# Local attention on one core: the projection moved behind a transpose and issued in two halves, the maxima one step earlier

## What is computed

```python
blk = mean of each 8 x 8 block                                   # 49 tokens
y_cmp = _mha(Q, blk, blk, ...); y_sel = _mha(Q, K_sel, K_sel, ...)   # K_sel: the 4 best blocks
# local attention: each pixel attends to its 7 x 7 neighbourhood
q = _lin(Q, wq_w[2], wq_b[2]);  k = _lin(patches, wk_w[2], wk_b[2]);  v = _lin(patches, wv_w[2], wv_b[2])
attn = softmax(einsum('bnhd,bnwhd->bnhw', q, k) * scale)
y_win = _lin(einsum('bnhw,bnwhd->bnhd', attn, v), pj_w[2], pj_b[2])
y = g[..., 0:1] * y_cmp + g[..., 1:2] * y_sel + g[..., 2:3] * y_win + Q
t = depthwise 3x3(_lin(y, pin_w));  x1, x2 = split(t)
out = _ln(y + _lin(gelu(x1) * x2, pout_w))
```

## Time and profile before

| | us |
|---|---|
| median of 3 runs | 847.04 (840.56 to 847.26) |
| the profiled execution | 846.81 |
| its span | 845.0 |
| TensorE busy | 715.2 (85%) |
| VectorE busy | 637.3 (75%) |
| ScalarE busy | 354.1 (42%) |
| GpSimd busy | 175.5 (21%) |

### The profile page before, as it was taken

How to read it: one execution, slowest core, us unless ns; L and a number is a source line. 1 busy time by engine, 2 the same in 40 slices (tenths; PEclk the granted TensorE clock), 3 DMA queues, 4 the chain that set the end, 5 groups by cost and what they waited for, 6 DMA issues and landing times.

```text
span 845.0 us, 14113 instructions
## 1 busy us (share of the span) xinstructions
PE 715.2 (85%) x5053; PEld 374.2 (44%) x5053; DVE 637.3 (75%) x1330; ACT 354.1 (42%) x609; POOL 175.5 (21%) x239
## 2 busy tenths in 40 slices
PE   4938976876589999987899899899979999999993
PEld 2525532333234444444455555455534545455551
DVE  6976545654679999986777777777749889999960
ACT  1170224434424343431455445445561251546566
POOL 1010122322325444340600000000240046600000
PEclk9966698999859999997799999999999999999998
DMA  5000055555479000002455665665100000000000
GB/s 223 0 1 0 18 135 132 138 143 142 125 195 243 4 0 1 2 0 73 113 146 158 157 170 140 168 168 140 38 4 1 0 0 1 1 19 20 38 39 38
DMA packets 52518, 66.21 MB, mean 78 GB/s; under 512 B 10590, under 2 KB 48226, under 8 KB 50594
## 3 DMA queue, kind: packets, MB, share of 16 engines
q1 hardware_dynamic: 49282, 43.08, 19.2%
q10 hardware_dynamic: 3168, 22.24, 9.7%
HBM read 43.03 MB, written 21.57 MB: 76 GB/s over the span
## 4 chain that ended last, share of the span: by engine, by line
PE 37%; DVE 21%; issue 6%; DMA 6%; ACT 4%; SPq 1%; POOL 0%; DVEq 0%; ACTq 0%
PE banks L853 12%; PE banks L793 5%; PE banks L777 4%; DVE mx L1224 4%; PE banks L755 4%; DVE sm L1237 4%; DMA Q<-nT 3%; PE banks L808 3%; DVE AC L1056 2%; DVE wn L1291 2%; DMA FP<-nT 2%; DVE X L1319 2%; DVE sm L1239 2%; PE banks L739 1%; DVE SEB L1227 1%
## 5 line engine op out<-in xcount | busy, mean ns | idle before, releaser
L955 ACT ACTIVATE P<-banks 126x480 f32<-126x480 f32 (+2 forms) x196 | 100.1, 520 | 127.2 <-PE banks L777 107.1
L853 PE MATMUL banks<-FP,PTB 128*128 128x392 f32 x384 | 129.2, 493 | 1.4 <-DVE c L1322 1.2
L1291 DVE TENSOR_REDUCE wn<-banks 128x4 f32<-128x728 f32 x112 | 101.7, 912 | 28.5 <-PE banks L755 27.3
L1056 DVE SCALAR_TENSOR_TENSOR AC<-XT,vec,AC 128x1540 f32<-128x1540 f32 (+5 forms) x48 | 115.1, 2401 | 1.1
L853 PEld LDWEIGHTS banks<-FP,PTB 128*128 128x128 f32 x384 | 72.8, 190 | 55.8 <-DVE c L1322 1.9
L501 POOL TENSOR_TENSOR SEB<-SEB,rg 112x392 f32<-112x392 f32 x112 | 58.3, 542 | 86.2 <-DVE rg L1244 86.2
L1153 DVE TENSOR_TENSOR pr<-pf,pk 128x434 f32<-128x434 f32 (+1 forms) x42 | 31.7, 756 | 58.4 <-ACT pk L910 57.8
L793 PE MATMUL banks<-P,Vw 126*17 126x120 f32 (+2 forms) x1568 | 74.4, 263 | 0.0
L485 POOL TENSOR_TENSOR pk<-pr,pk 128x434 bf16<-128x434 f32 (+1 forms) x42 | 42.7, 1018 | 137.5 <-DVE pk L1164 137.5
L934 ACT ACTIVATE SEB<-SEB 112x424 f32<-112x424 f32 x56 | 31.2, 557 | 85.7 <-DVE SEB L1227 83.9
L714 PE MATMUL banks<-PTB,VP 106*128 106x448 f32 x112 | 52.7, 558 | 5.1 <-ACT PTB L943 5.1
(11 more groups left out here) (227 smaller groups left out, 1249.9 us busy)
## 6 DMA issues: line engine op xcount, KB each, us to landing
k_parts<-pk SPq DMA_DIRECT2D x84, 108.5 KB, 2.8
Vw<-v_rows SPq DMA_DIRECT2D x84, 66.9 KB
q_parts<-pk SPq DMA_DIRECT2D x42, 112.0 KB, 2.7
K<-k_parts ACTq DMA_DIRECT2D x7, 651.0 KB, 5.9
v_rows<-vst SPq DMA_DIRECT2D x14, 263.5 KB
X<-in_x SPq DMA_DIRECT2D x2, 1568.0 KB, 8.3
out_y<-zs SPq DMA_DIRECT2D x8, 392.0 KB, 2.4
K<-k_parts ACTq DMA_DIRECT2D x7, 434.0 KB, 3.7
```

The source lines that it names most:

```text
L853: last = mm(bank(2 + place_in_unit, C, ZPIX), WT[:, dy, part, C * grp:C * (grp + 1)], D[:, part, QROWS * q + dy:QROWS * (q + 1) + dy, :].r ...
L955: a(P[q % 4][0:BKEYS[b], 0:4 * BQ[b]], PS[0:BKEYS[b], 4 + q % 2, 0:4 * BQ[b]], ACT.Exp).then_inc(sem("w_exp"), 1)
L1056: return ve.scalar_tensor_tensor(out=o, in0=src(ro + dy, rn, co + dx, cn), scalar=v(wcol + t), in1=o, op0=ALU.mult, op1=ALU.add)
L1291: ve.tensor_reduce(dst, src, AX.X, ALU.max, negate=True).then_inc(sem("w_slot_read"), 1)
```

## The change

LEAD goes from 12 to 13, so every A and every S, with its work on VectorE and its transfer on SP, comes one step earlier. D and Y stay at their steps. Because the entries of a step are listed with A and S ahead of Y, the step of Y now has A1 and S3 ahead of it. The first of the projection's two matmuls stays at the end of that step; the second is issued at the end of the next step, and it alone signals w_slot. The range of steps grows by one at each end.

```diff
-        LEAD = 12
+        LEAD = 13
...
-        STEP_RANGE = range(-LEAD, STEPS - STEPJ + Y_AT + 1)
+        STEP_RANGE = range(-LEAD, STEPS - STEPJ + Y_AT + 2)
...
                     if kind == "Y":
                         pe.wait_ge(sem("w_norm"), n + 1)
                         slot_free(order)
-                        for u in range(2):
-                            last = mm(PS[:, 2 * slot, 0:BAND], w("pj2", C, C * u), ON[:, u, :], start=(u == 0), stop=(u == 1))
-                        last.then_inc(sem("w_slot"), 1)
+                        mm(PS[:, 2 * slot, 0:BAND], w("pj2", C, 0), ON[:, 0, :], start=True, stop=False)
+                for kind, n, slot, order in pa.get(q - 1, ()):
+                    if kind == "Y":
+                        mm(PS[:, 2 * slot, 0:BAND], w("pj2", C, C), ON[:, 1, :], start=False, stop=True).then_inc(sem("w_slot"), 1)
```

## The result

The changed kernel takes 861.14 us (median of 4 runs, 856.33 to 866.23) against 847.15; the ratio is 1.0165, with a 95% interval of 1.0121 to 1.0208. It is slower. Its profiled execution took 859.87 (span 858.1), against 846.81 (span 845.0) before.

What follows compares the result with a forecast made beforehand. Local attention was taken as bound by TensorE issuing, plus waits for the residual add and tile 3's shift. Terms 7.7 + 0.8 - 0.4 + 0.5 = +8.6 us on about 847 gave 855.5, range 842 to 862.

Steps and rivals of the forecast that it cites:

- the likeliest case: Whole kernel: the author's own forecast of a slower kernel, 851 to 860 us, with 855.5 named; chance 0.55.
- the last full round's 0.7: Local attention: each of eleven rounds takes +0.7 us, 17.03 against 16.33, together +7.7.
- The order and its pairs: Two-slot ring: new order of entries, each waiting until VectorE has read the entry two places ahead.
- The waits: TensorE in one round: waits summing to 2.31 us on top of 14.66 us of issuing.
- What the biggest term rests on: Turn S1 waits 1.18 us for A4's reduction, as the reciprocals now run between A3's and A4's reductions.
- The shift: Tile 3's transfer, waited for at r8 before, arrives 2.5 us early; its wait had been covering VectorE's lag.
- The two halves: Projection issued as two halves: same matmuls, priced at VectorE's empty 1.9 us, already in the round's sum.
- The start: Two rounds before the eleven: +0.8 us (0 to +1.4); tile 2's shift leaving a step earlier: -0.4 (0 to -0.7).
- no cost: SP's queue: the sums' transfer leaves later but is wanted later, 5.1 us after issue against 5.0 before.
- The end: Last rounds of the local attention: the projection ends 0.6 us later, taken as +0.5 (0 to +0.8).
- The clock rival: TensorE's clock falls in one or two rounds, 2 to 3 us each, or RB lands late; 859 to 864, chance 0.12.
- The faster rival: VectorE keeps up, so turn S1 does not wait: rounds of 15.85 us, about 841 in all, chance 0.19.

Runs made afterwards that it cites:

- the second trace: The changed kernel, nothing altered, run and profiled once more beside the variants; 860.19 us, 1.0168 against the kernel before.
- the fastest one: The kernel before with the second maximum (A1) a step later, behind the turn S3, and the turn S1 a step later; 833.74 us, 0.9863.

## Why the prediction came out as it did

The measured 861.1 lies in the stated range (842 to 862), 0.9 us from its upper end and 5.6 above the 855.5; it is just past the likeliest case's own 851 to 860. The direction was right, and so was the mechanism in the rounds. The two ends of the stage were not: forecast at +1.6 together (0.8 - 0.4 + 0.5 and the last full round's 0.7), they cost 7.5 in both traces. The chances for slower by over 1% (0.40) and within it (0.48) put the measured outcome second.

**The order and its pairs: right.** The waits stand ahead of A1, S3, S0 and S1, where they were put, and for the releasers named.

**The waits: right to 0.16 each.** Forecast and measured: S3 0.57 and 0.50, S0 0.25 and 0.30, S1 1.18 and 1.10, A1 0.02 and 0.15. The two small ones ahead of Y's first half and A3 (0.16, 0.13) did not appear. The round: 17.03 and 17.08. Here two small errors cancel, which is luck: the waits come to 2.05 where the forecast had 2.31, and TensorE issues for 15.03 where it had 14.66. Ten of the rounds: 7.0 forecast, 7.5 measured.

**What the biggest term rests on: half right.** "Nothing hides the reciprocals once A3 is ahead of them" holds, but they are not the whole of S1's wait: moved ahead of A3 again, they take 0.54 off the round, and S1 still waits 0.55.

**The shift: right in the even rounds.** It is not waited for there in any kernel with another order than that of before. In the second round it is, in four of them (0.45 to 1.75). One experiment speaks for the sentence that the wait for the shift covered VectorE's lag: S3 moved alone takes it away, and S1 waits.

**The two halves: right in kind.** I put their price at VectorE's empty 1.9 us (measured 2.0) within the sum; alone they are 0.65 of a round's 0.74.

**The start: mis-sized.** The step said "+0.8, bounds 0 and +1.4" for the second round and "-0.4" for the start. The stretch to the first add grew by 4.0 and 4.9, of which 1.2 is work and 0.5 the next S3's wait, both moved across the cut by the order. The rest was taken too small because S1's and S3's waits came from the even rounds. In the first trace S1 waits 1.10 as forecast, but the transpose S3 waits 3.02 in the second round (413.64), against 1.79 before, behind two splits that stretched to 1.76 and 1.72 while GpSimd ran. In the second trace S3 waits 1.62 and S1 2.15, and slower matmuls cost 1.4. With S1 one step later the loss is gone, in the one trace of that kernel.

The sentence that the sums' transfer has 5.0 us before and 5.1 after, hence "no cost", holds in the even rounds (5.04 and 5.14 from issue to reciprocals). In the second round VectorE starts on the sums 4.1 us after their issue without a wait in the first trace, waits 0.96 for them in the second, and 3.28 with GpSimd out of the way. S1, now behind the reciprocals, hands this wait on to TensorE. It is a share of the second trace's loss and no part of the first's.

**The end: mis-sized.** "+0.5" and a full round's +0.7, together 1.2, were 3.6 and 2.65, with 1.2 us less work in them. The full round took 16.12 against 15.43, as forecast. In the drain TensorE waits for RB ahead of D:

```profile
629.26 0.93 PE L802 MATMUL banks<-RB,spread 128*128 128x448 bf16 x2 [1.71 <-DMA RB<-SB]
...
631.37 1.86 PE L807 MATMUL banks<-ON,W 128*128 128x448 f32 x2 [0.22 <-DVE ON L1310]
```

Before, the same wait was 0.86 and the projection's four passes took 1.77; here the first half alone takes 1.86, that is the 1.2 GHz level. The term took TensorE's work for the path. In the drain the path from the add over the six operations and RB to D is as long as before (7.76 us, 621.50 to 629.26, against 7.88, 611.33 to 619.21), and TensorE has S3 and r3's scores and products less to do in it (0.76), so its wait grows by 0.85. In all the traces of kernels with another order the granted clock of this interval or the one ahead of it is 0.79 to 0.91, with a wait of 1.60 to 3.24 us in one of the two; in the two with the order of before it is 1.00, with none over 0.86. That the longer wait brings the clock down is in line with this, but no run took the wait away alone: it stays argued.

**The clock rival: part of the outcome.** I gave it 0.12 and 2 to 3 us for each stretch, with 859 to 864 in all, and the measured 861.1 lies there. Of the third interval's 1.7 us more it cost 1.3; the other 0.3 are S1's longer wait, which is all that the second trace shows there. It cost most of the end and a part of the second trace's start, so my forecast and this rival came together, and the sum should have carried a term for it. Matmuls at the 1.2 GHz level follow a longer wait in the third interval: S1 waited 1.41 at 473.93, A6 at 475.43 took 0.72 instead of 0.50, and the next A 0.82. In the other nine rounds, with 1.10 at the same place, the clock stayed. It also stayed in the second trace behind the same wait of 1.41 (481.80), so the wait alone doesn't decide it.

```profile
465.00:482.00 17.00, 15.14 (x232) 8.37 (x230) 11.16 (x28) 7.09 (x16) 0.00 (x0) 0.90 0.52 137
482.00:499.00 17.00, 14.94 (x248) 8.51 (x246) 12.55 (x32) 8.35 (x17) 0.00 (x0) 1.00 0.53 140
```

(Windows of the changed kernel, columns as in the earlier trace rows; the granted clock is the column after GpSimd's.) At 0.90 TensorE was busy for longer and did 232 matmuls instead of 248, and VectorE 28 operations instead of 32.

**The faster rival fell**: S1 waits 1.10. Moved a step later it waits 0.45, under the 0.5 that the rival asked for, and the round is then 16.43, not its 15.85. One number of the text was misread: ScalarE is busy 7.91 of 16.20 in the round shown, not 7.82; nothing hangs on it.

What stays open: why the granted clock over the stage's first 30 us differs between the orders (0.77 before, 0.72 and 0.66 in the changed kernel, but 0.72 also in the kernel with LEAD 12 and S3 and S1 moved, and 0.83 in the fastest one), why VectorE starts one reduction late in the third interval, and what of the end's loss is cause and what effect of the clock.

## What to carry to other kernels

Before moving an entry of a two-slot ring, write down for each entry which one it then waits for and what the reading engine has in its queue between the two. A wait that goes away may have been the cover of another engine's lag: here it was VectorE's lag at S1. It came out at 0.43 once the wait for the shift was gone (only S3 moved), and the reciprocals between A3 and A4 made it longer (0.55 without them there, 1.10 with them). Splitting a product that one engine hands to another, with other work between the halves, delayed the whole here by about that work (0.65 a round, with 0.56 between the halves); keep it in one piece, and put the work that doesn't need it (here S3, or A1 for the slot) on the right side of it instead. And forecast the first and last rounds by themselves: in them other engines' work and other transfers stand on the path.

## What the runs showed of the hardware

- While GpSimd ran tensor operations on 128 x 768 elements (1.81 us each), VectorE's operations on 8 columns took up to 1.76 us instead of 0.17 and ended with GpSimd's. VectorE's reductions, which read PSUM, kept their 0.92 beside it. The Trainium skill (page SBUF — State Buffer, section "Who interferes with whom") says that an operation of VectorE with two inputs in SBUF contends with one of GpSimd that reads SBUF, that one in a two-port mode, which a cast can enter, and GpSimd's shut each other out for the whole instruction, and that a reduction never contends: the trace agrees. The same block of GpSimd's work in a full round cost 5.6 us in one kernel and 5.7 in the other; in the first two rounds its removal gave back 1.6 to 3.3.
- A 14 KB transfer between two places of SBUF (OB to SR, issued by SP) was in time in all the traces where VectorE came to it 3.5 us or more after its issue. Where VectorE had to wait for it, it started 3.3 to 4.5 us after the issue, and once 6.1 us (413.04 to 419.18, in the second round with GpSimd's work out of the way). The Trainium skill (DMA: Bandwidth & Descriptors, "Anatomy of one DMA — SWDGE (gpsimd) path") gives some 2.0 us of fixed time plus the bytes at 436 GB/s for its own path; by that this transfer would take about 2.03 us (an estimate), and the measurement decides otherwise here.
- TensorE's granted clock fell to 0.91 over one round of 18.73 us behind a wait of 1.41 us, and stayed at 1.00 behind the same wait in another trace of the same kernel.
